# Six buffers instead of four for the ternary weights' pieces in the first attention, and loads ahead of stores in its fourth turn

## The reference

```
x = x + tanh(g_xattn[0]) * image_attention(layernorm(x), ctx, ...)   # 16 heads of 32
x = x + tanh(g_ffn[0])   * quantised_ffn(layernorm(x), ...)          # ternary weights
x = x + tanh(g_xattn[1]) * cross_attention(layernorm(x), ctx, ...)   # 16 heads of 128
x = x + tanh(g_ffn[1])   * latent_attention_and_experts(layernorm(x), ...)
```

```
s = 1.0 / clip(mean(abs(w)), 1e-5)
w = clip(round(w * s), -1, 1) / s
```

## Time and profile before

| | us |
|---|---|
| median of 3 runs | 2243.73 (2242.27 to 2243.81) |
| profiled execution, device time | 2242.4 |
| its span, first to last instruction | 2240.7 |
| PE busy in the span | 2155.5 (96%) |
| DVE, ACT, POOL busy | 1315.1, 1083.3, 674.5 |
| mean granted clock of PE | 0.994 |
| `x_res<-b_w` on SP's queue | 48 loads of 512 KB |

### The profile page before, as it was taken

The page is one execution under the profiler, slowest core; times in us unless marked ns, Lnnn a source line. Parts: engine busy times, 40 slices in busy tenths (PEclk is TensorE's granted clock), DMA queues, the critical chain, the costliest instruction groups (busy, mean ns, idle before and its releaser), DMA issues. The chain is left out here.

```text
span 2240.7 us, 43433 instructions
## 1 busy us (share of the span) xinstructions
PE 2155.5 (96%) x18048; PEld 1796.3 (80%) x18048; DVE 1315.1 (59%) x2315; ACT 1083.3 (48%) x1919; POOL 674.5 (30%) x684
## 2 busy tenths in 40 slices
PE   7998899899999999999999999999899999999996
PEld 5766666454589999999999999999777877899996
DVE  7776676689854445444544454444555455767774
ACT  5676533578744444333433343433455554325553
POOL 4111110356412221111111111211354544135663
PEclk9999999999999999999999999999999999999998
DMA  7444302100033232321223123221000000258996
GB/s 282 151 148 140 95 6 114 57 1 1 29 132 123 76 113 95 113 76 64 87 95 113 57 95 120 70 73 57 25 2 2 2 2 30 85 188 265 272 280 105
DMA packets 46931, 215.32 MB, mean 96 GB/s; under 512 B 6160, under 2 KB 6160, under 8 KB 32400
## 3 DMA queue, kind: packets, MB, share of 16 engines
q1 hardware_dynamic: 29968, 139.13, 17.3%
q0 software_dynamic: 16768, 73.41, 11.4%
HBM read 169.00 MB, written 43.52 MB: 95 GB/s over the span
## 5 line engine op out<-in xcount | busy, mean ns | idle before, releaser
L343 POOL TENSOR_TENSOR c_prob<-c_prob,c_inv_mass 128x512 f32<-128x512 f32 x128 | 130.4, 1037 | 353.2 <-DVE c_inv_mass L335 353.2
L325 ACT ACTIVATE c_prob<-abc_banks,c_neg_peak 128x256 f32<-128x256 f32 x256 | 117.7, 472 | 177.6 <-DVE c_neg_peak L317 177.6
L50 PE MATMUL abc_banks<-bc_xt,bc_wq_hi 128*128 128x256 f32 x512 | 147.7, 288 | 0.0
L50 PE MATMUL abc_banks<-c_ctx,c_wk_hi 128*128 128x256 f32 x512 | 146.6, 286 | 0.0
L51 PE MATMUL abc_banks<-bc_xt,bc_wq_hi 128*128 128x256 f32 x512 | 144.9, 283 | 0.0
L52 PE MATMUL abc_banks<-bc_xt,bc_wq_lo 128*128 128x256 f32 x512 | 144.8, 283 | 0.0
L51 PE MATMUL abc_banks<-c_ctx,c_wk_hi 128*128 128x256 f32 x512 | 143.7, 281 | 0.0
L52 PE MATMUL abc_banks<-c_ctx,c_wk_lo 128*128 128x256 f32 x512 | 143.7, 281 | 0.0
L238 PE MATMUL abc_banks<-ab_wq,b_xqt 128*128 128x512 bf16 x512 | 118.7, 383 | 4.2 <-DVE b_h L209 2.2
L2196 DVE TENSOR_TENSOR c_v_lo<-abc_banks,c_v_hi 128x512 fp32r<-128x512 f32 x64 | 44.2, 691 | 133.1 <-ACT c_v_hi L2112 133.1
L1932 POOL DMA_DIRECT2D c_ctx<-kept_scratch x24 | 13.2, 550 | 347.0 <-PE abc_banks L52 347.0
(11 more groups left out here) (590 smaller groups left out, 7223.4 us busy)
## 6 DMA issues: line engine op xcount, KB each, us to landing
x_res<-b_w SPq DMA_DIRECT2D x48, 512.0 KB, 4.7
bc_xt<-kept_scratch POOLq DMA_DIRECT2D x24, 1024.0 KB, 5.1
c_ctx<-kept_scratch POOLq DMA_DIRECT2D x24, 1024.0 KB, 5.2
e_raw<-e_w SPq DMA_DIRECT2D x15, 1536.0 KB
bc_raw<-c_w SPq DMA_DIRECT2D x16, 1024.0 KB, 4.9
h_res<-e_w SPq DMA_DIRECT2D x7, 1536.0 KB
kept_scratch<-bc_xt SPq DMA_DIRECT2D x8, 1024.0 KB, 3.8
kept_scratch<-c_ctx SPq DMA_DIRECT2D x8, 1024.0 KB, 4.0
```

The lines of the kernel that those rows point to most:

```text
L50: pe.matmul(out, lhs[0], rhs[1], start=first, stop=False)
L325: ins = act.activation(self.prob[:, u % 2, j, :], self.s_ps[:, j, :], ACT.Exp, bias=self.neg_peak[:, u % 2, j:j + 1], accum_out=self.mass[ ...
L343: pool.tensor_tensor(part, part, self.inv_mass[:, u % 2, js].unsqueeze(2).to_broadcast([P, 2, SEQ]), ALU.mult).then_inc(self.prob_done, 1)
```

## The change

It has three parts. The buffers for pieces become six: two more lie in the two halves of `early_raw`. The first load into each of these waits for `w_lo_done[WV]`. The ring of a turn runs over all buffers that x has not taken: six in turns -1 to 1, five in turn 2, four in turn 3. And in turn 3 `load_piece(k)` comes before `store_piece(k - 2)`, as in the turns before.

```diff
+    BUFFERS = 6
...
-        piece_in, piece_out = [sem(f"piece_in{r}") for r in range(4)], [sem(f"piece_out{r}") for r in range(4)]
+        piece_in, piece_out = [sem(f"piece_in{r}") for r in range(BUFFERS)], [sem(f"piece_out{r}") for r in range(BUFFERS)]
...
-        buffer_of, users, later = [], [0] * 4, []
+        buffer_of, users, later = [], [0] * BUFFERS, []
         for i, n in STEPS.items():
+            first = max(i - 1, 0)
             for p in range(n):
-                r = p % 4 if i < 2 else (1 + p % 3 if i == 2 else 2 + p % 2)
+                r = first + p % (BUFFERS - first)
                 buffer_of.append(r)
...
         def piece(k):
 
-            at = 2 * TB * TB + TB * buffer_of[k]
+            r = buffer_of[k]
+            if r >= 4:
+                return early_raw[:, r - 4, :, :].rearrange("p j s -> p (j s)")
+            at = 2 * TB * TB + TB * r
             return x_res[:, at:at + TB, :].rearrange("p t d -> p (t d)")
...
                 earlier = [j for j in range(k) if buffer_of[j] == r]
+                if r >= 4 and not earlier:
+                    sp.wait_ge(w_lo_done[WV], 1)
                 if earlier and earlier[-1] < PIECES:
...
                     k = first + p
-                    if i < 3:
-                        load_piece(k)
+                    load_piece(k)
                     if k - PIECES >= 2 and p >= 2:
                         store_piece(k - 2)
-                    if i == 3:
-                        load_piece(k)
                     if p == STEPS[i] // 2:
                         load_context(i + 3)
```

## The result

| | before | after |
|---|---|---|
| median of 8 runs, us | 2243.86 (2242.27 to 2249.56) | 2229.94 (2228.49 to 2240.96) |
| profiled execution, us | 2242.4 | 2229.9 |
| its span | 2240.7 | 2228.2 |
| mean granted clock of PE | 0.994 | 0.995 |
| instructions in the profile | 43433 | 43433 |

The ratio of the times is 0.9938, with a 95% interval of 0.9923 to 0.9953. That is 13.9 us less, with an interval of 10.5 to 17.3. The forecast was 14.33 us less and a time of 2229.4. Both kernels run the same number of instructions; what has changed is when they run.

The account below looks back on a forecast made before the run. PE, busy 96%, can gain only where idle or at a lower clock, here turn 3: 60.98 - 46.65 = 14.33 us (10.48 idle, 3.85 clock), so 2243.73 - 14.33 = 2229.4 us; range 2225 to 2235.

Parts of the forecast that it names:

- The chain in SP's queue in turn 2: Turn 2's tail: load k stands behind store k-3, which waits for rounding k-3; no wait was expected for pieces 38 to 40.
- With L = 4.1: Turn 2's tail: L is the time of a piece's load from issue until ACT starts on it, taken as 4.1 us.
- up to 2 us later: Piece 37 in turn 2: lands at 184.0, or up to 2 us later behind the next context's 512 KB.
- the sum of 4.47 us against 4.62: Turn 2's tail: a store's issue of 0.37 us plus a load of 4.1, just under ACT's two pieces, 2 x 2.31.
- The slack: End of turn 2: ACT done at 193.3 but may end at 195.9 before PE wants the peaks; 2.6 us of cover.
- the late loads of x keep their place: SP's queue: late loads of x stay behind the last store of a turn, listed among parts that cost or bring nothing.
- the second stall: Turn 3, PE before its outputs at 245.03: 4.46 us, released by GpSimd's low output part, to shrink to 0.44.
- first stall: Turn 3, PE before 202.91: 6.46 us, released by ACT's copy of the peaks, expected to vanish.
- The parts counted at nothing: Load 4's wait on GpSimd, short cover for loads 8 and 32, sum-piece waits (3.4 us), late x: counted as 0.
- rival 1: Transfers take the place of the wait: loads land later, with 7.5 us 4.5 of the gain go, 2234 us; chance 0.10.
- Rival 2: Waits were not what held PE; ACT or GpSimd late from their own work, gain near 0, 2243 us; chance 0.03.
- Rival 3: Short look-ahead where a turn begins: loads 8 and 32 late, 12 us slower, 2256 us; chance 0.03.

Follow-up runs that it names:

- the two halves: Two runs of the changed kernel: turn 3 put back to two buffers and store ahead of load, 2235.47 us; turn 2 put back to three buffers, 2238.04 us.

## Why the prediction held, and where it was off

**What bounds the stage.** Right. The waits for pieces were what held PE, in two places with a cause each, as the two halves show.

**The chain in SP's queue in turn 2.** Right in kind: a load no longer waits for an old store's landing. One size was off. "With L = 4.1" was read from loads that went out 4.6 to 4.8 us apart. In the changed kernel they follow each other faster, beside stores and the context. Piece 37 took 6.2 us, just over the "up to 2 us later" that the prediction gave, and the trace has pieces 38 and 39 landing 6.2 and 5.8 us after their issue at 181.73 and 184.07. Only piece 40 (issued at 188.95) landed within 4.1 us, in 3.7. So the sum of 4.47 us against 4.62 did not hold for 38 and 39. That they show no wait is partly luck: piece 37 had made ACT 1.95 us late already, and with piece 37 in time piece 38 would have come some 1.6 us after it was wanted (an estimate: landed at 187.9, wanted at 184.04 + 2.31 = 186.35). Either way it stays inside the slack of 2.6 us.

**The slack.** The prediction named one user of ACT's tail, the peaks, and gave 2.6 us of cover. The scores indeed did not wait, though the peaks came 3.1 us after the mark and not 0.9 (195.41 - 192.34). The step that failed is "the late loads of x keep their place": they keep it in the queue, and so move with the last store. This cost 0.51 us, the difference of 47.12 and 46.61, which the run with the stores three behind gave back.

**Turn 3.** Right: load 45 is out at 217.80, in time, the second stall is 0.45 us, output_high comes 38.35 us after the mark where 37.85 was expected. The prediction told of four buffers and of the order as one thing. The run with the store first has the order worth 6.1 us in its profiled execution and the two buffers without it 0.7, and the run with five buffers shows that three buffers are enough for that stall.

**The sum.** 14.33 was forecast for the turn and 13.86 measured. The term that was off is the 46.65 taken for the new turn 3: it measured 47.12, and 46.61 once x was in time too. The split was forecast as 10.48 idle and 3.85 clock, and measured as 9.93 and 3.93. So the clock was sized well, and the idle time falls short by the wait of the late x. The figure by the Trainium skill's rule (TensorE: Matmul & The Clock Gate, Part 1), 4.9 us for the clock, is too high here, and the trace shows why: from 196.50 to 202.91, where PE stood idle in its first stall, the granted clock was 0.86, so 0.14 x 6.41 = 0.9 us of the 4.9 lay where PE had nothing to do. The profiled execution moved by 12.5 us and not by 13.86, because its last stage took 1.2 us longer, well inside the 10 us over which that stage spreads from one profile to another.

**The parts counted at nothing.** Right but for the late x. Load 4 went out at 24.94 for the wait on GpSimd, pieces 8 and 32 had no wait, and the waits of turn 0 went without moving the mark of turn 1 (98.74 in both).

**The rivals.** ACT's waits sum to 2.3 us (under 3 was the sign) and PE's longest in the stretch is 0.99 (1 was the bound). The transfers did take longer, as in rival 1, but at 6.2 us at most and not 7.5. Rival 2 falls with the halves. Rival 3's short look-ahead did not show.

## What to carry to other kernels

When a ring of buffers is short, find out what the next load stands behind: the landing of an old store (a buffer cures that) or a younger store in the same in-order queue (only the order cures that). Here the order was worth 6.1 us of turn 3 in the profiled execution, and the extra buffers alone 0.7. Then follow everything that stands behind the late item in that queue to its own user, for the slack of the first user is not that of the others. And price a stall of PE with the clock that goes with it: 9.9 us of idle time cost 13.9. Last, a transfer's time read from a queue that waits much is too short for one that waits less: 4.1 us became 6.2.

## What the runs showed of the hardware

How long a DMA of one queue took to land changed with what was issued around it. The 512 KB load of piece 37 took 4.1 us when it went out 2.4 us behind another of 512 KB (before), and 6.2 when it went out 0.5 us behind it, with a store and a further load following within 2 us (after). A 256 KB store, 2.6 us at the median, took about 5.5 between a megabyte of loads ahead of it and a load behind it (182.20 to 187.76 in the run with five buffers). The runs do not tell apart what the transfers ahead and those behind added.

After a wait of 1.26 us on PE (five buffers) the granted clock stayed at 1.00, that is 2.4 GHz throughout, and PE's busy time in the turn was 45.19 us against 45.17. After one of 3.69 us (store first) it was 0.94 over the turn, the first matmul of 512 columns took 0.79 us in place of 0.50, and the busy time was 47.66 us. So the small stall cost only itself, and the larger one 2.5 us more than itself.
